# A fused attention and mixture-of-experts block: experts' outputs moved to token columns and summed in one PSUM bank

## The reference, cut to what matters

```python
x = x + tanh(g_xattn) * attention(layernorm(x), ctx, ctx)      # 16 heads of 64, causal
def ffn(xn, rw, W1, W2):                                       # W1 128x256, W2 256x128
    h = xn * rsqrt(mean(xn * xn) + RMS_EPS) * rw
    return silu(h @ W1) @ W2
xf = layernorm(x).reshape(448, 128)
gates = softmax(xf @ router_w)                                 # 14 routed experts
masked = top 2 of gates, divided by their sum (+ 1e-9)
routed = sum over e of masked[:, e] * ffn(xf, rms_w[e], w1[e], w2[e])
shared = ffn of 2 shared experts, summed with weight 1
x = x + tanh(g_ffn) * (routed + shared)
```

## Time and profile before

| what | us |
|---|---|
| three timed runs: median (lowest to highest) | 121.04 (120.91 to 121.61) |
| the profiled execution's own time | 121.5 |
| its span, first to last instruction | 119.7 |
| PE busy | 108.7 (91% of the span) |
| DVE busy | 68.8 |
| ACT busy | 59.7 |
| POOL busy | 43.9 |

### The profile page before, as it was taken

How to read it: one execution, slowest core, us unless ns; L and a number is a source line. 1 busy time by engine, 2 the same in 40 slices (tenths; PEclk the granted TensorE clock), 3 DMA queues, 4 the chain that set the end, 5 groups by cost and what they waited for, 6 DMA issues and landing times.

```text
span 119.7 us, 2370 instructions
## 1 busy us (share of the span) xinstructions
PE 108.7 (91%) x814; PEld 92.0 (77%) x814; DVE 68.8 (58%) x194; ACT 59.7 (50%) x100; POOL 43.9 (37%) x75
## 2 busy tenths in 40 slices
PE   6979999994999999999785989999999999999980
PEld 6867768652478478478484979999999999999980
DVE  0058966669469769869524435999733333333361
ACT  4053778833739579579581569423333323333300
POOL 7703598000000100100100758666666666664000
PEclk9999999999679999999999999999999999999999
DMA  3999999999993000000000000000000000000002
GB/s 93 266 299 344 407 411 417 415 430 435 427 418 132 3 0 0 0 5 0 0 0 0 5 0 5 3 0 3 0 5 0 0 0 0 0 0 0 0 0 77
DMA packets 3169, 13.76 MB, mean 115 GB/s; under 512 B 431, under 2 KB 1007, under 8 KB 2775
## 3 DMA queue, kind: packets, MB, share of 16 engines
q1 hardware_dynamic: 3159, 13.63, 30.2%
HBM read 13.40 MB, written 0.23 MB: 114 GB/s over the span
## 4 chain that ended last, share of the span: by engine, by line
PE 72%; DVE 11%; ACT 7%; DMA 4%; issue 3%; DVEq 0%; ACTq 0%
PE score_ps L723 15%; PE attn_ps L723 7%; PE attn_ps L611 6%; PE ring L716 6%; PE ring L718 5%; PE ring L717 5%; PE ring L585 5%; PE score_ps L542 5%; DMA wkq_space<-in_wkq_dram 4%; PE ring L483 3%; PE ring L511 3%; ACT square_junk L803 3%; PE ring L513 2%; PE ring L512 2%; PE score_ps L536 2%
## 5 line engine op out<-in xcount | busy, mean ns | idle before, releaser
L924 ACT ACTIVATE mixT<-ring 128x896 f32<-128x896 f32 x16 | 14.6, 918 | 26.9 <-PE ring L718 26.9
L723 PE MATMUL score_ps<-w,mixT 128*112 (+1 forms) x160 | 19.1, 273 | 0.2 <-ACT mixT L924 0.2
L723 PEld LDWEIGHTS score_ps<-w,mixT 128*112 128x112 f32 x160 | 18.7, 177 | 0.8 <-issue 0.3
L436 POOL TENSOR_TENSOR h_scale<-h_base,minus_half 112x1 f32<-112x1 f32 x4 | 2.2, 549 | 43.9 <-DVE h_base L1055 43.9
L611 PEld LDWEIGHTS attn_ps<-wkq_space,mixT 128*112 128x112 f32 x128 | 14.5, 179 | 3.5 <-issue 3.5
L1195 DVE SCALAR_TENSOR_TENSOR xn_rows<-score_ps,gates,xn_rows 112x128 f32<-112x128 f32 x36 | 10.2, 345 | 11.5 <-PE score_ps L723 11.3
L611 PE MATMUL attn_ps<-wkq_space,mixT 128*112 128x128 f32 x128 | 15.3, 277 | 0.5 <-ACT mixT L795 0.5
L716 PE MATMUL ring<-hT_hi,w_hi 128*128 128x448 f32 (+2 forms) x36 | 13.9, 385 | 1.5 <-issue 1.4
L401 POOL TENSOR_TENSOR w_full<-w,columns 128x256 f32 (+1 forms) x16 | 9.8, 614 | 12.2 <-PE ring L718 10.5
L718 PE MATMUL ring<-hT_hi,w_lo 128*128 128x448 f32 (+2 forms) x36 | 12.6, 350 | 0.0
L717 PE MATMUL ring<-hT_lo,w_hi 128*128 128x448 f32 (+2 forms) x36 | 12.6, 349 | 0.0
(11 more groups left out here) (133 smaller groups left out, 187.1 us busy)
## 6 DMA issues: line engine op xcount, KB each, us to landing
ctx_all<-in_ctx_dram SPq DMA_DIRECT2D x4, 1500.0 KB, 18.7
w<-in_w_dram SPq DMA_DIRECT2D x2, 1792.0 KB, 27.0
wkq_space<-in_wkq_dram SPq DMA_DIRECT2D x2, 512.0 KB, 5.6
wvo<-in_wvo_dram SPq DMA_DIRECT2D x1, 1024.0 KB, 9.8
w<-in_w_shared_dram SPq DMA_DIRECT2D x2, 256.0 KB, 15.9
ctx_head<-in_ctx_head_dram SPq DMA_DIRECT2D x1, 480.0 KB, 7.9
ctx_headT<-in_ctx_headT_dram SPq DMA_DIRECT2D x1, 224.0 KB, 4.8
x_space<-in_x_rows_dram SPq DMA_DIRECT2D x1, 224.0 KB, 5.1
```

The lines of the kernel that those rows point to most:

```text
L723: last = nc.tensor.matmul(dst, hidden[slot][:, c, t * ROWS:(t + 1) * ROWS], w2_chunk(c), start=(c == 0), stop=(c == 1))
L924: nc.scalar.activation(hidden[slot], ring[:, 2 * slot:2 * slot + 2, 0:TOKENS], ACT.Silu).then_inc(S["hidden_ready"], 1)
```

## The change

What the new kernel does:

- **Token columns.** The output matmuls now take w2 as the stationary operand and all 448 tokens as moving columns. All experts but the last add up in one PSUM bank (`out_sums`), without DVE; the last goes to two half banks. `x1` is transposed on PE and added once at the end; the output is written as 128 x 448 and transposed back on the host.
- **Gates on the hidden values.** A gate is now a row of values, one for each column. The 448 x 14 gates are transposed on PE, copied by DVE (`gatesT`), stored to DRAM, and read back broadcast to 128 partitions in five groups of experts (`GATE_GROUPS`). DVE multiplies each routed expert's hidden values (128 x 896) by its tile of gates. tanh(g_ffn) goes into w2 for the shared experts.
- **Split.** Experts 0 to 3 (`WHOLE`) use plain float32 for the output product: two matmuls of 448 columns. Experts 4 to 15 (`PARTED`) use hi and lo of hidden values and w2: six fp32r matmuls of 448 columns. ACT rounds the gated values (`round_hidden`, 128 x 896), DVE subtracts (`subtract_hidden`, 128 x 896). There are 8 slots of hidden values and 4 of hi and lo.
- **POOL** scales and splits all 16 W1 and splits 12 W2, most of it during the attention pairs, in pieces that each wait for a pair's `probs_ready`; the four `h_scale` powers stand between these pieces. The weights are loaded in groups of four into space that is free by then, so SP's list now has waits; `ctx_all` has room for four batches and is loaded twice.
- **PE's order of the experts**: hidden 2, output 0, hidden 3, output 1, x1 transposes, hidden 4 and 5, gates' transposes, hidden 6 to 9; then output e and hidden e+8 in turn. The loop is written out.
- **Head**: A0 is folded and emptied ahead of A1. Six warming products follow each of the two P0 transposes (`FIRST_PRODUCTS`).
- **Last pair**: job C3.0.1 is emptied by DVE; batch 7's squares come before C3; the guard's transposes come before `attention_out(3)`, and PE loads the flag between its two halves; DVE's `subtract_hi(0)` comes behind the guard.

The diff, cut to its core:

```diff
+WHOLE = [0, 1, 2, 3]
+PARTED = [e for e in range(EXPERTS) if e not in WHOLE]
+FULL_SLOTS = 8
+PART_SLOTS = 4
+GATE_GROUPS = [(0, 1), (1, 2), (2, 4), (4, 8), (8, ROUTED)]
...
+            sp.wait_ge(S["gatesT_ready"], 1)
+            sp.dma_start(gates_dram, gatesT).then_inc(S["gates_stored"], 16)
+            sp.wait_ge(S["gates_stored"], 16)
+            for n, (a, z) in enumerate(GATE_GROUPS):
+                sp.dma_start(gate_tiles[:, a:z, :], gates_dram[a:z, :].partition_broadcast(P))\
+                    .then_inc(gates_loaded[n], 16)
+            for n, cols in enumerate(halves):
+                sp.wait_ge(S["result_ready"], n + 1)
+                sp.dma_start(out[:, cols], result[:, cols]).then_inc(S["stored"], 16)
...
+            def split_w1(experts):
...
+                    nc.gpsimd.tensor_scalar(w1_full[:, :], first_weights(e), rms_cols[:, e:e + 1], None,
+                                            ALU.mult).then_inc(S["w1_full_ready"], 1)
+                    pool.wait_ge(S["w1_full_ready"], e + 1)
+                    nc.gpsimd.tensor_copy(w1_hi[:, e, :], w1_full[:, :])\
+                        .then_inc(S["w1_hi_ready"], 1)
+                    pool.wait_ge(S["w1_hi_ready"], e + 1)
+                    nc.gpsimd.tensor_tensor(w1_lo[:, e, :], w1_full[:, :],
+                                            w1_hi[:, e, :].bitcast(FP32), ALU.subtract)\
+                        .then_inc(S["w1_scaled_ready"], 1)
...
+            split_w1(range(SHARED))
+            pool.wait_ge(S["probs_ready"], 2)
+            split_w1(range(SHARED, 7))
+            pool.wait_ge(S["probs_ready"], 4)
+            split_w1(range(7, 12))
+            second_scale(0)
+            pool.wait_ge(S["probs_ready"], 6)
+            split_w1(range(12, EXPERTS))
+            split_w2([4])
+            second_scale(1)
+            pool.wait_ge(S["probs_ready"], 8)
...
+            second_scale(2)
+            split_w2(range(5, 10))
+            second_scale(PAIRS - 1)
...
+            pool.wait_ge(S["logits_ready"], 1)
+            split_w2([10, 11])
+            pool.wait_ge(S["gatesT_ready"], 1)
+            split_w2(range(12, EXPERTS))
...
+            def output_parted(e, sums, cols=slice(0, TOKENS)):
...
+                for c in range(2):
+                    nc.tensor.matmul(sums, w2_hi[:, n, c, :], hi[:, c, cols],
+                                     start=(alone and c == 0), stop=False)
+                    nc.tensor.matmul(sums, w2_lo[:, n, c, :], hi[:, c, cols],
+                                     start=False, stop=False)
+                pe.wait_ge(S["hidden_lo_ready"], n + 1)
+                for c in range(2):
+                    last = nc.tensor.matmul(sums, w2_hi[:, n, c, :], lo[:, c, cols],
+                                            start=False, stop=(e >= EXPERTS - 2 and c == 1))
...
+            for e in range(4, FULL_SLOTS + SHARED):
+                silu(e)
+            for e in range(FULL_SLOTS + SHARED, EXPERTS):
+                round_hidden(PARTED[e - FULL_SLOTS - SHARED])
+                silu(e)
+            for e in PARTED[EXPERTS - FULL_SLOTS - SHARED:]:
+                round_hidden(e)
...
+            for e in range(SHARED, EXPERTS):
+                gate_hidden(e)
+                if e - 1 in PARTED:
+                    subtract_hidden(e - 1)
+            subtract_hidden(EXPERTS - 1)
+            dve.wait_ge(S["x1T_ready"], 1)
+            dve.wait_ge(S["expert_done"], EXPERTS - 1)
+            then_wait(nc.vector.tensor_tensor(result[:, :], out_sums, x1T, ALU.add))
+            for n, cols in enumerate(halves):
+                dve.wait_ge(S["half_done"], n + 1)
+                nc.vector.tensor_tensor(result[:, cols], result[:, cols], last_sums[n], ALU.add)\
+                    .then_inc(S["result_ready"], 1)
```

More of the change, by code:

```diff
@@ new lines, in split_w2 @@
+            def split_w2(experts):
+                for e in experts:
+                    n = PARTED.index(e)
+                    weights = second_weights(e).rearrange("p (c d) -> p c d", c=2)
+                    pool.wait_ge(w2_loaded[n // 4], 16)
+                    nc.gpsimd.tensor_copy(w2_hi[:, n, :, :], weights)\
+                        .then_inc(S["w2_hi_ready"], 1)
+                    pool.wait_ge(S["w2_hi_ready"], n + 1)
+                    nc.gpsimd.tensor_tensor(w2_lo[:, n, :, :], weights,
+                                            w2_hi[:, n, :, :].bitcast(FP32), ALU.subtract)\
+                        .then_inc(S["w2_split_ready"], 1)
@@ L496, in fold_values @@
                 fold(n, "M", lambda rows, c: wvT[rows, c, :], lambda rows, c: wo[rows, c, :])
-            fold_keys(0)
+            pe.wait_ge(wkq_loaded[0], 16)
+            for g in range(2):
+                for i in range(4):
+                    rows = slice(HEAD * g, HEAD * g + HEAD)
+                    c = head_of(g, i) // 2
+                    last = nc.tensor.matmul(ring[:, bank_of(f"A{g}"), i * D:(i + 1) * D],
+                                            wkq[rows, 0, 0, c, :], wkq[rows, 0, 1, c, :],
+                                            start=True, stop=True)
+                last.then_inc(S["ring_filled"], 1)
             keep_warm(FOLD_PRODUCTS, misc_ps[:, 0:P])
@@ L733, in static_w2, with next_hidden, output_whole @@
-            def static_w2(e):
-                return lambda c: w2[:, e, c, :]
+            def next_hidden(e):
+                pe.wait_ge(S["hidden_ready"], e - 1)
+                hidden_products(e).then_inc(S["hidden_filled"], 1)
+            def output_whole(e):
+                if e < SHARED:
+                    pe.wait_ge(S["w2_shared_scaled"], e + 1)
+                    pe.wait_ge(S["hidden_ready"], e + 1)
+                else:
+                    pe.wait_ge(S["w2_whole_loaded"], 16)
+                    pe.wait_ge(S["hidden_gated"], e - SHARED + 1)
+                for c in range(2):
+                    last = nc.tensor.matmul(out_sums, w2_whole[:, WHOLE.index(e), c, :], hidden(e)[:, c, :],
+                                            start=(e == 0 and c == 0), stop=False)
+                last.then_inc(S["expert_done"], 1)
@@ L1190, in wide @@
                 return col[:, :].unsqueeze(2).to_broadcast([ROWS, PAIRS, ROUTED])
-            def add_expert(place, gate, before=moe):
-                for t in range(PAIRS):
-                    last = nc.vector.scalar_tensor_tensor(
-                        out=moe[:, t, :], in0=out_banks[place][0:ROWS, t * D:(t + 1) * D],
-                        scalar=gate(t), in1=before[:, t, :], op0=ALU.mult, op1=ALU.add)
-                last.then_inc(S["acc_done"], 1)
-            def static_gate(e):
-                return lambda t: gates[:, e, t:t + 1]
             dve.wait_ge(S["logits_filled"], 1)
```

391 lines of the change are left out of this document (218 added, 173 removed).

## The result

The changed kernel takes 126.49 us (median of 4 runs, 125.75 to 127.36) against 121.19 for the kernel before, a ratio of 1.044 with a 95% interval of 1.036 to 1.052. It is slower; the forecast was 117.6. One kernel can run in a faster or a slower state, so every ratio here is one of fast runs alone, while medians and ranges are of all runs. The profiled execution took 126.18 with a span of 124.4, to be set beside the 119.7 of before and the 116.3 that the sum gave.

A forecast was written before the change was run, and what follows sets the result against it. The prediction took PE to bound the expert stage, moving to DVE, and a loop through all engines the attention stage. Span 117.8 + 0.3 + 0.5 - 0.4 - 1.6 - 0.3 = 116.3 against 119.7; median 117.6, range 115.4 to 120.8.

The forecast's parts named there:

- (4): Attention stage: POOL's splits at T = 1.75 us make the h_scale power 0.5 late; cost 0.5, bounds 0 and 4.4.
- rival C: Attention stage: POOL too slow, costing 9T - 15.2; at T = 2.2 span 120.5, median 121.8; chance 0.12.
- Two signs that the prediction named for being wrong: Of three signs: gate products starting later than 84 us, POOL's tensor_scalar taking 0.6; the third concerned PE's lower clock.
- terms named for the lower end of the range: Whole kernel: no coupling, guard at its full gain, gates at 3.4; given as 115.4.
- Head: Start of attention: A0 folded alone is ready 0.9 us earlier, about 0.65 remains, 0.4 counted as gain.
- Clock at 31 us: Attention stage: the 12 warming products keep PE's clock from falling to 0.5 at 31 to 34 us, gaining 1.6.
- Last pair: End of attention: earlier flag loading removes PE's 1.37 us wait from the residual; net gain 0.3, bounds 0 and 0.9.
- Gates: Before gated experts: gates at 78.1, copied by 80.6, store 1.8 and load 2.4 through DRAM, ready at 84.9.
- rival B: Gates' round trip through DRAM: 6.5 instead of 4.2, 2.3 us more, 119.9; chance 0.11.
- Experts: Expert stage: DVE becomes the bound, 26 operations at 1.05, 27.3 us; coupling to PE through ACT costs 1.4.
- rival A: PE's clock: dip at 31 us stays (+1.6) or falls in last experts (+1.5); either 119.2, both 120.7; chance 0.22.
- POOL against DVE: Expert stage: POOL's w2 splits reach 1 us into DVE's gate products; 0.3 added.

The follow-up runs named there:

- e1: Changed kernel with POOL's order alone changed: h_scale powers earlier, w2 splits last, some POOL waits left out; 120.55 us.
- e2: Changed kernel, same order, with POOL's W1 scaling written as tensor_tensor with a repeated column instead of tensor_scalar; 121.24 us, ratio 0.9998 to the kernel before.
- e6: Changed kernel with only the first power, h_scale(0), moved behind the split of expert 7; 126.98 us, ratio 1.047 to the kernel before.
- e3: Changed kernel with early h_scale powers and tensor_tensor scaling together, w2 splits re-placed; 116.92 us, ratio 0.968 to the kernel before.
- e4: e1 without the 12 warming products in the first pair (FIRST_PRODUCTS = 0); 119.8 us, ratio 0.986 to the kernel before.
- e7: e5 with the gates of the first three routed experts spread by PE instead of through DRAM; 119.91 us, ratio 0.993 to the kernel before.
- e5: e3 with ten hidden buffers for eight, the two more in mixT; 116.77 us, ratio 0.963 to the kernel before.
- e8: e7 with eight hidden buffers again and the orders of PE and ACT rewritten for the PE spreads; 114.36 us, ratio 0.945 to the kernel before.

## Why the prediction was wrong, and where it was right

**The step that failed is (4) of the attention stage, "POOL".** It had two faults. The first is a size: "As a one-input instruction I put it at 0.4 like the cast". The `tensor_scalar` took 0.92 at the least and 0.95 in the mean, so T was 0.92 + 0.40 + 0.73 and the gaps, 2.31 (the first split of pair 0 starts at 27.47, the next at 29.78), not 1.75. That lies outside both bounds, since I had taken 0.61, the form of the earlier trace rows, for the upper end; nothing in the trace of before bounded a form it did not hold. The second is in the model. The splits of experts 2 to 6 must be done between the probabilities of pairs 0 and 1, too; at T = 1.75 they just fit (5 x 1.75 = 8.75 in 8.94), and I priced only what comes after. At 2.31, and with a few instructions stretched, that group ended at 39.6, some 3.4 us late, and the next five start behind it. With this term, 5T - 8.94, added to rival C's 9T - 15.2, T = 2.31 gives 2.6 + 5.6 = 8.2 us in place of the 0.5 in the sum.

The residual was to stand at 65.24 + 0.5 - 0.4 - 1.6 - 0.3 = 63.4 and stood at 72.2, 8.8 later. The rows give POOL 10.4 us in place of the 0.5: DVE's waits for two powers, 7.2 and 0.5; PE at its lower clock after standing still, 1.7; and DVE instructions stretched beside POOL, some 1.0. Against that stands 1.1 us more than forecast from the last pair (below). The 8.2 come near to it in part by luck: they put 5.8 on the first power and 2.4 on the second, and have no term for the clock or for the stretched instructions. Rival C named the right mechanism and place, at 12%, and its price was less than half of the real one. Two signs that the prediction named for being wrong came: `tensor_scalar` took 0.92, beyond the 0.6, and the gate products started at 92, not by 84.

Two sums of the prediction do not come out. The terms named for the lower end of the range give 117.6 - 1.4 - 0.6 - 0.8 = 114.8 and not 115.4, and the upper bound of step (4) is 4.7, as under rival C, and not 4.4. Neither matters here: 126.5 us lies above the upper end of the range, and POOL's cost above both bounds.

e1 (order) takes away all of the residual's lateness and e2 (form) 4.3 of its 10.0 us, e6 shows that it is a backlog and not one misplaced instruction, and e3 with both comes to a span of 115.1, 1.2 below the forecast's 116.3. So the rest of the sum held as a whole. In the attention stage it did by errors that cancel: e3's last residual, 62.94, is where the forecast without the 0.5 for POOL has it, with the last pair 1.1 us better and DVE's `probs<-probs,row_inv` stretched to as much as 1.02 us. Term by term:

- **Head.** First `row_max` at 17.87 (18.34 before), the last probabilities of pair 0 at 26.75 (27.15): 0.4, as forecast.
- **Clock at 31 us.** The dip is gone in the profile (1.00 in each microsecond from 30 to 35), and its cost is 1.66 (e4 against e1) for the 1.6 forecast. That the products removed it is not shown (e4). What I had not seen is that one kernel's mean clock differs from run to run, so that a median moves by less.
- **Last pair.** The first hidden product follows the attention at once, the 1.37 of the earlier trace rows is gone. From the last residual but one to the last it takes 72.23 - 64.38 = 7.85 us (e1 and e4: 7.86 and 7.87), where the kernel before took 65.24 - 55.97 = 9.27:

```profile
55.97 0.34 DVE L1038 SCALAR_TENSOR_TENSOR x<-attn_ps,tanh_col,x_space 112x128 f32<-112x128 f32 x1
```

So the edits of the last pair gain 1.4, where I took 0.3 out of bounds of 0 and 0.9. Which of them (the guard's place, the flag, C3.0.1 on DVE, batch 7's squares) gives it was not tried.

- **Gates.** Forecast: the first gate product 84.9 - 65.24 = 19.7 us after the residual. Measured 92.02 - 72.23 = 19.8, but of two errors that cancel: the gates themselves were there after 12.0 (84.21; 12.9 forecast), and store and loads took 5.1 (4.2 forecast, within 3.4 and 6.5). So rival B cost 0.9 of its 2.3.
- **Experts.** From the first gate product to the end 32.4 (32.9 forecast). DVE's 14 and 12 operations take 1.084 and 1.089 as forecast, but follow each other by 1.005, not 1.05; the coupling through ACT costs 1.85 in the changed kernel where I had 1.4 and 0.3. PE's work by expert was right (2.43 us while hidden products remain).
- **Clock in the last experts (half of rival A).** It stayed at 1.00, with PE busy for 8.43 of the 10 us from 109 to 119.
- **POOL against DVE.** POOL's last split ends at 91.6, before the first gate product, so 0 instead of 0.3. In attention `probs<-probs,row_inv` went from 625 ns to 690 in the mean, 0.5 us over eight of them, and `xn_rows` took 0.56 and 0.61 where it had taken 0.34. The waits for `probs_ready` did not keep POOL away from these products, as I had written: once it is late, it works through them.

## What to carry to other kernels

Price an instruction by its form, not by its operand count: where the trace has no row of that form on that engine, the bound must reach well past the nearest form, and the form that the trace does have is the safer choice. When an idle engine is given work between the steps of a loop, write out the time by which each small result behind that work is due, from the first period on, and put the small result first; a backlog does not vanish by moving one of them. And a head start for one engine is worth only what the written orders of the engines behind it let through: e7 lost 3.1 us against e5 with nearly the same instructions with which e8 won 2.4.

## What the runs showed of the hardware that I had not expected

- On POOL, 128x256 float32 times one column takes 0.92 us as `tensor_scalar` and 0.61 as `tensor_tensor` with the column repeated, the cast 0.40. The Trainium skill (GPSIMD Engine Reference, "Engine selection") says that one-input operations are roughly at line rate there. For the cast that fits (1037 ns for 1024 columns, where DVE takes 1.04 ns a column). For `tensor_scalar` with a column as its scalar, if it is counted as one-input, the trace disagrees, and the trace decides.
- Single POOL instructions are stretched in the attention stage: 1.17 instead of 0.92 and 0.82 instead of 0.40 (at 34.38 and 35.62 us in the changed kernel). Both overlap DVE's `probs<-probs,row_inv` (34.06 to 34.76, 35.56 to 36.18), and the first of these is itself stretched (0.70 for 0.62). That the one delays the other is read from the overlap; no run separates it. It adds 0.7 us to that group of five splits.
- A small store to DRAM and the load that spreads it over 128 partitions cost 5.1 us from the copy of the gates to the first use (store issued at 86.92, loads issued at 88.43, first product at 92.02). Spread by PE (e8), the three rows take 0.91 to 1.01 us each, 0.75 to 0.86 apart, and the first product starts 1.6 us after the copy.
- The same kernel gets a granted clock of 1.0 in one execution and 0.96 to 0.98 in another, with more than 1 us between them (e1: 118.2 and 119.5 to 122.1; the kernel before at 0.996 or more 119.5 to 120.3, else 120.9 or more). Where a change is to remove one dip, count runs by their clock and do not rely on one profile.
